# A Perceiver-like stack on one core: the 16-head attention outputs of layers 1 and 3 turned by VectorE in 32x32 blocks

## The reference, cut to what matters

```python
def _L3_xattn_ref(x, y, Wq, bq, Wk, bk, Wv, bv, W1, b1, W2, b2):   # L3x; y: 64 x 128 keys x 96
    q = (x @ Wq + bq).reshape(B, N, 16, 8)
    k = (y @ Wk + bk).reshape(B, M, 16, 8)
    v = (y @ Wv + bv).reshape(B, M, 16, 8)
    attn = jax.nn.softmax(jnp.einsum('bnhd,bmhd->bhnm', q, k) / np.sqrt(8), axis=-1)
    out = jnp.einsum('bhnm,bmhd->bnhd', attn, v).reshape(B, N, 128)
    return jax.nn.relu(out @ W1 + b1) @ W2 + b2
```

## Time and profile before

| what | value |
|---|---|
| median of 3 runs | 2758.32 us (2748.19 to 2759.39) |
| the profiled execution | 2753.47 us, its span 2752.2 us |
| PE busy | 2412.4 us (88%) |
| DVE, ACT, POOL busy | 1664.2 (60%), 1388.0 (50%), 779.1 us (28%) |
| granted TensorE clock, mean | 0.955 |
| waves of L1a, first scores to last product | 703 to 921 us |
| waves of L3x | 1892 to 2324 us |

### The profile page before, as it was taken

How to read it: one execution, slowest core, us unless ns; L and a number is a source line. 1 busy time by engine, 2 the same in 40 slices (tenths; PEclk the granted TensorE clock), 3 DMA queues, 4 the chain that set the end, 5 groups by cost and what they waited for, 6 DMA issues and landing times.

```text
span 2752.2 us, 63312 instructions
## 1 busy us (share of the span) xinstructions
PE 2412.4 (88%) x27087; PEld 1615.5 (59%) x27087; DVE 1664.2 (60%) x4680; ACT 1388.0 (50%) x2371; POOL 779.1 (28%) x684
## 2 busy tenths in 40 slices
...
DMA packets 50458, 84.23 MB, mean 31 GB/s; under 512 B 9536, under 2 KB 24768, under 8 KB 49792
## 3 DMA queue, kind: packets, MB, share of 16 engines
q1 hardware_dynamic: 50176, 80.18, 10.5%
...
## 4 chain that ended last, share of the span: by engine, by line
PE 57%; DVE 21%; ACT 10%; issue 6%; POOL 4%; DMA 2%; SPq 1%; DVEq 0%; POOLq 0%; ACTq 0%
PE psum L917 6%; PE psum L879 4%; PE psum L875 4%; PE psum L1570 3%; PE psum L456 3%; PE psum L448 2%; PE psum L1560 2%; PE psum L1961 2%; PE psum L1663 1%; PE psum L1953 1%; DVE c_L3x_most L1705 1%; PE psum L1364 1%; PE psum L1414 1%; DVE c_L2x_mx L2058 1%; PE psum L1415 1%
## 5 line engine op out<-in xcount | busy, mean ns | idle before, releaser
L456 PE MATMUL psum<-halves_held 128*128 128x512 bf16 x655 | 192.9, 405 | 7.5 <-DVE c_L2x_p L2064 7.5
L864 POOL TENSOR_TENSOR c_L3f_h<-c_L3f_h,c_L3f_spread 128x512 f32<-128x512 f32 x96 | 120.6, 1277 | 127.5 <-DVE c_L3f_h L907 65.5
L907 DVE TENSOR_TENSOR c_L3f_h<-c_L3f_h,psum 128x512 f32<-128x512 f32 (+1 forms) x112 | 75.8, 684 | 108.3 <-PE psum L879 80.5
L893 ACT ACTIVATE c_L3f_h<-psum 128x512 f32<-128x512 f32 (+1 forms) x112 | 64.8, 595 | 128.1 <-PE psum L875 109.7
L917 PEld LDWEIGHTS psum<-weights,c_L3f_h 128*128 128x128 f32 (+1 forms) x896 | 107.3, 191 | 19.3 <-issue 18.2
L917 PE MATMUL psum<-weights,c_L3f_h 128*128 128x128 f32 (+1 forms) x896 | 110.5, 276 | 0.0
L456 PEld LDWEIGHTS psum<-halves_held 128*128 128x128 bf16 x655 | 60.4, 102 | 85.3 <-issue 35.5
L864 POOL TENSOR_TENSOR c_L0f_h<-c_L0f_h,c_L0f_spread 128x512 f32<-128x512 f32 x64 | 80.0, 1273 | 94.1 <-DVE c_L0f_h L907 55.6
L879 PE MATMUL psum<-c_L3f_xT,weights 128*128 128x512 f32 x208 | 106.2, 596 | 0.0
L875 PE MATMUL psum<-c_L3f_xT,weights 128*128 128x512 f32 x208 | 105.9, 595 | 0.0
L1705 DVE TENSOR_REDUCE c_L3x_most<-psum 128x16 f32<-128x2048 f32 x32 | 73.2, 2289 | 40.7 <-PE psum L1560 40.6
...
## 6 DMA issues: line engine op xcount, KB each, us to landing
...
```

The costliest lines, as they stand in the source:

```text
L456: nc.tensor.matmul(j.psum[:, bank, :], j.half["ident"], j.half["take"], start=True, stop=True)
L864: nc.gpsimd.tensor_tensor(h, h, j.m["spread"][:, f, :], ALU.mult).then_inc(*j.up("mixed"))
L907: nc.vector.tensor_tensor(h, h, j.psum[rows, bank, 0:j.tok], ALU.mult).then_inc(*j.up("gated"))
```

## The change

The product with the values writes its 64 columns as two runs of 32, so that each 32x32 block of PSUM holds one group's heads and 32 tokens. VectorE then turns all blocks of the two banks (one bank in L3x) in one instruction, `nc.vector.transpose`, from PSUM to `oT`, now with tokens on the partition. Reciprocal and product read SBUF. A second such instruction turns `att` back, by blocks, straight into `xT`. The features of `xT` then stand in another order, and the rows of `wo` (L1a) and `W1` (L3x) are laid out in that order on the host (`by_lane`, a change of layout). ACT's copies (L1690, L1693, and L464 for `att`), PE's transposes (L1670, and L448 for `att`) and their steps are gone. The next wave's scores wait for `o_turned`, that is for the first transpose alone. `PLAN` is the same; `ORDER` is new from its first letter to its last.

```diff
 def pe_waves(nc, j, keys):
         if w:
-            pe_warm(nc, j, 2)
-            t.wait_ge(*j.at("att", w))
+            pe_warm(nc, j, 0)
+            t.wait_ge(*j.at("o_turned", w))
...
-                            put = t.matmul(out, m["va"][k, t_, h, :], m["pT"][k, col:col + S], start=True, stop=True)
+                            put = t.matmul(out.rearrange("p (b c) -> p b c", b=2)[:, :, g * LANE:(g + 1) * LANE], m["va"][k, t_, h, :],
+                                           m["pT"][k, col:col + S].rearrange("p (b c) -> p b c", b=2), start=True, stop=True)
         put.then_inc(*j.up("out"))
-        yield
-        pe_warm(nc, j, 0)
-        t.wait_ge(*j.at("outT", w + 1))
-        for u in range(tiles):
-            for g in range(QUAD):
-                put = t.transpose(psum[:, u if tiles == 2 else 3, g * P:(g + 1) * P], m["oT"][:, u, g * P:(g + 1) * P], j.c["ident"])
-        put.then_inc(*j.up("o_turned"))
...
 def dve_divide(nc, j, w, tiles):
+    v.wait_ge(*j.at("out", w + 1))
+    v.transpose(out, j.psum[:, 2:2 + tiles, :].rearrange("p a c -> p (a c)")).then_inc(*j.up("o_turned"))
+    yield
     v.wait_ge(*j.at("o_turned", w + 1))
-    v.reciprocal(z, out[:, :, :, WIDTH]).then_inc(*j.up("denom"))
+    v.reciprocal(z, lane_blocks(out)[:, :, WIDTH]).then_inc(*j.up("denom"))
     yield
     v.wait_ge(*j.at("denom", w + 1))
-    v.tensor_tensor(m["att"][:, w * tiles:(w + 1) * tiles, :].rearrange("p u (h d) -> p u h d", h=HEADS),
-                    out[:, :, :, 0:WIDTH], bcast(z, 3, WIDTH), ALU.mult).then_inc(*j.up("att"))
+    v.tensor_tensor(att.rearrange("p (b d) -> p b d", d=WIDTH), lane_blocks(out)[:, :, 0:WIDTH], bcast(z, 2, WIDTH),
+                    ALU.mult).then_inc(*j.up("gained"))
+    yield
+    v.wait_ge(*j.at("gained", w + 1))
+    xT = m["xT"][:, w * tiles * P:(w + 1) * tiles * P].rearrange("p (u r q) -> p r u q", u=tiles, r=2)
+    v.transpose(xT, att.rearrange("p (r u q) -> p r u q", r=2, u=tiles)).then_inc(*j.up("att"))
...
 def pe_L1a(nc, j):
-    pe_warm(nc, j, 2)
+    pe_warm(nc, j, 0)
     t.wait_ge(*j.at("att", 2))
-    pe_turn(nc, j, 2, m["att"])
-    yield
-    pe_warm(nc, j, 3)
-    t.wait_ge(*j.at("features", 2))
     pe_project(nc, j, 3, m["xT"])
...
 ORDER = (
-    "dddlQqPADdkdDDLDdpapapKPaDDvdDVggLGlpppvvAaPAPGPPvvdvVVkQqqppaaAVVDVdgpaKgpppPPvvadvdAAPAGlGPPPvvdkdDDVppDVdAaapapgpgpVd"
+    "qddDDpdvldDVkqQLdpDKQDPDdDaagpPaApgALpGpPvvdaAvPGlPvPvVpdVkqapagApVapgdpVDVKpdQdlPvvDadvAPAGPvAvkqdpddapPgaPGlPdDpDVVAaV"
```

More of the change, by code:

```diff
@@ L68, in by_head, with by_lane @@
     return out.reshape(P, 256)
+def by_lane(w):
+    return np.ascontiguousarray(w.reshape(4, 4, 8, w.shape[1]).transpose(1, 0, 2, 3)).reshape(P, w.shape[1])
 def weight_table():
@@ L1541, in room_attention, with lane_blocks @@
             "pT": r.tile("pT", P, 2048), "oT": r.tile("oT", P, P // keys, BANK), "z": r.tile("z", P, 2, HEADS), "att": r.tile("att", P, 4, D)}
+def lane_blocks(ap):
+    return ap.rearrange("p (b c) -> p b c", c=LANE)
 def room_turned(r, keys):
@@ L1656, in pe_waves @@
                                 k = slice(64 * r, 64 * r + 64)
-                                t_, out = w * tiles + u, psum[LANE * n:LANE * n + ONE, 2 + r, (u * QUAD + g) * S:(u * QUAD + g + 1) * S]
+                                t_, out = w * tiles + u, psum[LANE * n:LANE * n + ONE, 2 + r, u * 256:(u + 1) * 256]
                                 col = (g * 2 + u) * 256 + n * S
@@ L1686, in act_waves @@
                          psum[:, 2 * half:2 * half + 2, :], ACT.Exp, scale=WIDTH ** -0.5).then_inc(*j.up("exp"))
-        yield
-        s.wait_ge(*j.at("out", w + 1))
-        if tiles == 2:
-            s.copy(m["oT"][:].rearrange("p u (g r q) -> p r (u g) q", g=QUAD, r=2),
-                   psum[:, 2:4, :].rearrange("p r (n q) -> p r n q", q=S)).then_inc(*j.up("outT"))
-        else:
-            s.copy(m["oT"][:, 0, :], psum[:, 2, :]).then_inc(*j.up("outT"))
 def dve_waves(nc, j, keys):
@@ L1701, in dve_waves @@
         v.wait_ge(*j.at("scores", w + 1))
-        if w:
-            v.wait_ge(*j.at("att", w))
         for u in range(tiles):
@@ L1724, in dve_divide @@
     v, m = nc.vector, j.m
-    bank = 0 if tiles == 2 else 3
-    out = j.psum[:, bank:bank + tiles, :].rearrange("p u (h e) -> p u h e", h=HEADS)
-    z = m["z"][:, 0:tiles, :]
+    n = tiles * HEADS
+    out = m["oT"][:].rearrange("p u c -> p (u c)")
+    z = m["z"][:].rearrange("p u h -> p (u h)")[:, 0:n]
+    att = m["att"][:].rearrange("p t d -> p (t d)")[:, w * tiles * P:(w + 1) * tiles * P]
+    v.wait_ge(*j.at("out", w + 1))
+    v.transpose(out, j.psum[:, 2:2 + tiles, :].rearrange("p a c -> p (a c)")).then_inc(*j.up("o_turned"))
+    yield
     v.wait_ge(*j.at("o_turned", w + 1))
-    v.reciprocal(z, out[:, :, :, WIDTH]).then_inc(*j.up("denom"))
+    v.reciprocal(z, lane_blocks(out)[:, :, WIDTH]).then_inc(*j.up("denom"))
     yield
     v.wait_ge(*j.at("denom", w + 1))
-    v.tensor_tensor(m["att"][:, w * tiles:(w + 1) * tiles, :].rearrange("p u (h d) -> p u h d", h=HEADS),
-                    out[:, :, :, 0:WIDTH], bcast(z, 3, WIDTH), ALU.mult).then_inc(*j.up("att"))
+    v.tensor_tensor(att.rearrange("p (b d) -> p b d", d=WIDTH), lane_blocks(out)[:, :, 0:WIDTH], bcast(z, 2, WIDTH),
[4 more added lines that the diff above has]
+    v.transpose(xT, att.rearrange("p (r u q) -> p r u q", r=2, u=tiles)).then_inc(*j.up("att"))
 def dve_lanes(nc, j, out, src, lanes, done, of="lane4"):
@@ L2083, in pe_L3x @@
     yield from pe_waves(nc, j, SC)
-    yield
-    t.wait_ge(*j.at("att", 4))
-    pe_turn(nc, j, 3, m["att"])
     for f in range(2):
@@ L2089, in pe_L3x @@
         if f == 0:
-            t.wait_ge(*j.at("features", 2))
+            pe_warm(nc, j, 3)
+            t.wait_ge(*j.at("att", 4))
         t.matmul(psum[:, f, :], j.weight("w1")[:, f * P:(f + 1) * P], m["xT"][:], start=True, stop=True).then_inc(*j.up("inner"))
@@ new lines @@
+    "PKDDpVdVDVLpVLpaVapaVVpDaGpVpGPpAKPvvPkdpPddAlPAPaApAvvaPavaPvPpVVPvAPdVAVVApAVvvkDvPvKvvvVgv9pgPapVVVpaVpaVpaVVpaGplVpd"
+    "DPpAkPvvPADpDdALPadLPdDAlpAGvDvaPavKPvPaPpVVPvA3PVdAVVApAVvvvPvvvvVgv8pgPaKDpVVDVpVpVapDaVpVaGkpVpaGPpAPvvPAdpPadpPbrPrr"
+    "rprArrAprrArdrPlrrprLrarPrarrrDvcPbKspVpVsvPaDpAsPvdPk+sppsapgvpagcgPBRpDgRcAacRRRRPRDVLPARRRpRvPRgRRpRARcRaRRvpRDVgCvpB"
+    "gSpacvSPgPSVcASccSPvGPVGpAPaGPVpGPbrGrPrrpAArdpapvrParVprVGPrrrGrprdrrCrvCrrPrrcpbAsCKCsCavCsVpGsCadCspVgpDgvpPgcAaplPag"
@@ new lines @@
+    "PPBRPRRRcRDARARpRRRcRRvcRgRRPVpRRRRPRaDVCvpBdgScvpgSpakcSvPgAScLcSPvGVPAdGpVPaGCAPGPVpGPbrrCdrrrpDrrrCdarrArPrKrrrpVPAvG"
+    "CrVrpGrrrcpbasPvpAsCaPsCVspGCsvCgpVgpPgpAaPvcDgpBRDRPRRaRcRvPRDRLRpRRRgpRaRRApRRPRvaRgpRVDClPBScpSpaAPSVcvSdPvgkcgAcVGcP"
+    "GcAGPvPqdddpVlPaSGAPKVPGppbCrrrPrrarprArrAprrrrCrrPrrrdVCrGrpPvcVAPbGasCVdCGvsCddlCspCapVpQDgvPdpAgskpagsPavpgPvBRpRRcRR"
+    "aRRpRRRDcRvgRpRDRpgaAcvLpgpRaRcRDRvcRgRcdPDDCVPBScAkcSPvPdSvpPdaqVpdvlpadSkpdGASpaVagKGvCadPgCAGvPvDdPgVPAPCAlvPVGvppVaP"
@@ new lines @@
+    "LapGPaAPGpACvPDVvdCGaVCGKCvvCDpVaQPvPAVpAV+DPakDDdPAPAGLpAvqdpGpVaadpVVvGpapagV1PaVPvAgPADA2PvdvDgDVVAv6pvpVaDpVLa2PalDK"
+    "pAVKPvdvdAaPVdPDQPDAdvAlvPkdDpdAVDkGPvLPADaVDpAGapvDqpVpaVdaGpdDKdpapagVV1PavPPvAgAA5PlvdvdgVVdAdlv9pVVLpa2PavkApVaDDPA1"
+    "PKpVdPvPAAPvDVaDPPAvvADGpAavGkVpLVdaVGpvqdppadDapKVQpdValgPPAPADpaDADdvLvPaVgVvAvgVDV9PAv1pkDVpavPadpAPaVKQDPpdAPvPAdvDl"
+    "aVPDLPAvvAdDGpAavGkVpVda2pVGvqdppaapVpVavDgPaPPADAdpdvAlKdDPaVgVLvAvgkVV8PAv2pVDvPadpApaPaVKdPpAPvPAdvDQlaDPdDdPDAvvAVpG"
```

139 lines of the change are left out of this document (60 added, 79 removed).

## The result

The changed kernel takes 2651.26 us (median of 4 runs, 2643.88 to 2657.0), the one before 2756.88 us beside it. The ratio is 0.9621, 95% interval 0.9588 to 0.9654: faster by 105 us, where 30 were forecast. The profiled execution took 2657.0 us, its span 2655.7.

A forecast was written before the change was run, and what follows sets the result against it. TensorE was taken as the engine to relieve, each wave being a loop through three engines. Between 37 us and 19 us, 30 us was taken off 2753.47; with half of a 4.8 us offset added, 2726 us, range 2695 to 2764 us.

The forecast's parts named there:

- The rest of the order: The ten other blocks do the same work in a new order: costed at nothing, with 12 us either way.
- The sum for the waves: Waves of L1a and L3x: 37 us gained by shorter waits between steps, 19 us by the chain of waits; 30 us taken.
- the links: Steps between waves and in each job's last wave, L1a and L3x: 74 us shorter over both contexts, half elapsed, 37 us.
- Removed work: Transposes and copies of L1a, L3x and `att` gone: 49.6 us off TensorE, 44 us off ScalarE.
- Gain 1.1 to 1.8, I take 1.3 us: Between two waves of L3x, product with the values to next scores: 1.3 us shorter, in 24 waves.
- If TensorE's order lets each context use what it gains: Condition on the 37 us elapsed gain in the waves; rows of the order were read as mostly meeting it.
- The chain argument: Waves: half of the work removed, 47 us, shows in the time, less half of VectorE's added work, 28 us: net 19 us.
- B: Rival, more than the sum: L3x's wave period falls from 6.5 to 5.2 us, 59 us gained with L1a, 2697 us; chance 0.14.
- the sign that was set for C: An unchanged period of 6.5 us from wave to wave in L3x.
- C: Rival, hidden anyway: in L3x VectorE's maxima end last, so TensorE's relief there is worth nothing; 2748 us; chance 0.15.
- D: Rival, slower: VectorE's transposes in L1a and L3x cost like its dear operations, or the new order is worse elsewhere; 2805 us; chance 0.11.
- The mark set at the end: Forecast is wrong if time goes or comes in blocks without this kind of attention: then the order did it, not the transposes.

The follow-up runs named there:

- e7: The kernel before, transposes still on TensorE, with the new order everywhere but in the waves of L1a and L3x: 2687.68 us, ratio 0.9725 to the kernel before.
- e11: The changed kernel with each first VectorE transpose written twice: 2693.6 us, ratio 0.9733 to the kernel before.
- e1: The changed code, transposes on VectorE, with the order of before throughout: 2804.44 us, ratio 1.0167 to the kernel before.
- e6: The changed kernel with the 108 filling matmuls of L1x and L1f left out, order as it is: 2665.99 us, ratio 0.9638 to the kernel before.

## Why the prediction was off

**The step that failed is "The rest of the order. ... I cost that at nothing, with 12 us either way".** It measured 74 us (e7), in L0a, L0f, L1x and L1f, where TensorE's waits became shorter and its granted clock higher. The bound was the flaw: it was made from the cost of the filling matmuls, so it bounded only how much filling could differ and not how long TensorE waits for others. The rows that speak against it were in the profile of before: 12 us of idle TensorE in L0f, 53 in L1x and 14 in L1f, at granted clocks of 0.98, 0.92 and 0.93.

**The sum for the waves held, in part by luck (see the links).** Removed work: no L1670, L1690 or L1693 of before is left. TensorE's busy time fell by 85.5 us on the pages, 49.6 were forecast; but the changed kernel's trace lacks 134 filling matmuls. e11 has the same TensorE instructions in the same order and a trace with all of them: 2362.6 us, 50 us less than before, as forecast. VectorE's rose by 41 us and not by 50 to 60: the new instructions are 60 us, and those that both kernels have read 19 us shorter in sum, spread over the whole program.

**Links.** "Gain 1.1 to 1.8, I take 1.3 us" between two waves of L3x: the distance from product to next scores fell by 2.2 us in the median, and in L1a by 2.9 where 1.8 was taken. That is more than forecast, as the scores also moved ahead in TensorE's order. It is within 1.5 us in 21 of the 32 waves, before in none; the 4.2 us that the forecast read from one wave were not typical of L3x. In a job's last wave the distance from the product to the output matrix fell by 2.8 us in L3x and 2.5 in L1a in the mean, where 1.6 and 2.0 were taken. All 48 links together became some 117 us shorter over both contexts, where the sum had 74. The elapsed time is near the forecast all the same: 16 us less in L3x (20 forecast), 18 in L1a (12 forecast). So 34 of 117 us is less than a third, and not the half that was taken: the links were sized too low and their share too high, and the two nearly cancel. That is luck.

**"If TensorE's order lets each context use what it gains"** was the condition, and it was the whole of it: without the waves' new order the turning loses 50 us (e1). The forecast named the condition and gave it no price. The chain argument, "half of what comes to VectorE", is near for L3x and too low for L1a (e11).

**The rivals.** B (2697 us, loops closer to TensorE's limit) came nearest in time, for a reason that is wrong: where both contexts are in waves of L3x the period did not fall to 5.2 us. The same mark, first scores to first scores of any context, goes over 2038.3 to 2079.1 us in six steps before and over 2022.4 to 2062.9 in six steps after, 6.8 us either way. So the sign that was set for C is there in that stretch; that the maxima are what ends last there was not tested. The 16 us came at its two sides: from the first wave's scores to the ninth's it is 136 us before and 128 after, over the next 15 waves 126 and 127, from there to the last wave's scores 157 and 150. D fell with the transposes' price. The row of the shuffle in the earlier trace rows, 0.730 us, was the best guide to the 0.716 us of the transpose of 128x512. The forecast read it wrongly: it is 1.43 ns a column, not the 1.2 ns of the copy, so the two don't "agree on about 1.2 ns an element at both sizes". The 311 ns of the Trainium skill (VectorE: DVE Perf Modes, The three transpose paths) for 128x128 in bf16 is what `att` takes here in fp32 (311 ns); the estimate of 1.24 us made from it by four was too high against the 0.716 us measured, as one instruction pays its start once.

**The mark set at the end did its work**: "wrong if the time goes or comes in blocks without an attention of this kind: then the order did it". It deserved a chance of its own in the list of rivals, in both directions, and had none but a clause in D.

**What stays open.** Why L0f and L1x wait less is shown as which waits went or shrank, not as which step's move in the string removed each; for L0a and L1f not even that. How much of the gain outside the waves the higher clock gives was tested in L1x alone, and there together with the filling (e6). Whether the new turning with the old wave order in new surroundings loses, as e1 does in the old ones, was not tried.
